# A shifted-window transformer block: attention output as one group per band in shared banks, both copies behind the second group, and a new order on all engines

## What is computed

```python
h = _ln(x, g1, b1)                                   # over the 128 channels
h = jnp.roll(h, (-3, -3), axis=(1, 2))
xw = _win_part(h)                                    # windows of 49 tokens
q, k, v = split(xw @ w_qkv + b_qkv)                  # 4 heads of 32
attn = einsum('whnd,whmd->whnm', q * 32 ** (-0.5), k)
attn = softmax(attn + bias[None] + MASK, axis=-1)    # relative bias, mask of the shift
out = einsum('whnm,whmd->whnd', attn, v) @ w_proj + b_proj
x = x + roll(_win_rev(out), (3, 3))
h2 = _ln(x, g2, b2)
h2 = gelu(h2 @ w_fc1 + b_fc1) @ w_fc2 + b_fc2        # 128 -> 512 -> 128
return x + h2
```

## Time and profile before

| | us |
|---|---|
| median of three runs | 3138.68 (3138.0 to 3142.47) |
| the profiled execution's own time | 3140.98 |
| its span, first to last instruction | 3139.2 |
| PE busy | 2989.0 (95%) |
| DVE busy | 2907.3 (93%) |
| ACT busy | 2255.3 (72%) |
| POOL busy | 1385.2 (44%) |

### The profile page before, as it was taken

How to read it: one execution, slowest core, us unless ns; L and a number is a source line. 1 busy time by engine, 2 the same in 40 slices (tenths; PEclk the granted TensorE clock), 3 DMA queues, 4 the chain that set the end, 5 groups by cost and what they waited for, 6 DMA issues and landing times.

```text
span 3139.2 us, 119115 instructions
## 1 busy us (share of the span) xinstructions
PE 2989.0 (95%) x51984; PEld 2732.5 (87%) x51984; DVE 2907.3 (93%) x7463; ACT 2255.3 (72%) x4480; POOL 1385.2 (44%) x775
## 2 busy tenths in 40 slices
PE   5999999999999999999999999999999999999998
PEld 3888888988888888889888888988888898888887
DVE  7999999999999999999999999999999999999995
ACT  3777777777777777777777777777777777777775
POOL 2444444444444444444444444444444444444442
PEclk9999999999999999999999999999999999999999
DMA  1111111111111111111111111111111111111110
GB/s 54 33 33 33 33 43 33 33 40 37 33 35 42 33 33 33 44 33 33 40 37 33 33 43 34 33 33 44 33 33 42 35 33 33 40 36 34 33 28 22
DMA packets 217571, 111.78 MB, mean 36 GB/s; under 512 B 15095, under 2 KB 216791, under 8 KB 217047
## 3 DMA queue, kind: packets, MB, share of 16 engines
q1 hardware_dynamic: 216899, 104.14, 13.0%
q10 hardware_dynamic: 147, 0.02, 0.0%
HBM read 52.73 MB, written 51.38 MB: 33 GB/s over the span
## 4 chain that ended last, share of the span: by engine, by line
PE 59%; DVE 29%; ACT 9%; issue 3%; SPq 0%; DMA 0%; POOL 0%; POOLq 0%; DVEq 0%; ACTq 0%
PE psum L767 13%; PE psum L725 7%; DVE xn L556 7%; PE psum L692 6%; PE psum L727 5%; PE psum L726 5%; DVE scores L576 5%; PE psum L699 4%; PE psum L746 4%; PE psum L753 4%; PE psum L707 3%; PE psum L720 3%; PE psum L732 3%; ACT probs L356 3%; DVE stream L590 3%
## 5 line engine op out<-in xcount | busy, mean ns | idle before, releaser
L318 POOL TENSOR_TENSOR rstd<-ve,minus_half 112x7 f32<-112x7 f32 x256 | 380.3, 1486 | 1251.7 <-DVE ve L551 1251.7
L767 PE MATMUL psum<-wfc,hT 128*112 128x128 f32 x7168 | 803.5, 273 | 1.5 <-ACT hT L410 1.5
L767 PEld LDWEIGHTS psum<-wfc,hT 128*112 128x112 f32 x7168 | 791.2, 177 | 2.1 <-issue 2.1
L410 ACT ACTIVATE hT<-psum,bias_h 128x392 f32<-128x392 f32 x1024 | 573.7, 599 | 233.0 <-PE psum L727 232.9
L314 POOL TENSOR_TENSOR probs<-probs,row_inv 128x784 f32<-128x784 f32 x256 | 383.7, 1521 | 470.7 <-DVE row_inv L585 470.7
L576 DVE TENSOR_TENSOR scores<-scores,row_max 128x784 f32<-128x784 f32 x256 | 447.5, 1748 | 8.8
L725 PE MATMUL psum<-x2T_hi,wfc_hi 128*128 128x392 f32 x1024 | 405.6, 396 | 28.0 <-DVE stream L590 25.8
L590 DVE TENSOR_TENSOR stream<-psum,stream 112x384 f32<-112x384 f32 (+1 forms) x512 | 303.9, 602 | 97.2 <-PE psum L753 83.3
L556 DVE TENSOR_SCALAR xn<-stream,mean,rstd 112x128 f32<-112x128 f32 x896 | 375.4, 476 | 1.6 <-POOL rstd L318 1.6
L321 POOL TENSOR_TENSOR stream<-stream,brow_fc 112x896 f32<-112x896 f32 x128 | 360.3, 2815 | 5.6 <-DVE xn L556 5.6
L402 ACT ACTIVATE kT<-psum,bias_k 128x392 f32<-128x392 f32 x256 | 150.8, 589 | 289.0 <-PE psum L732 285.6
(11 more groups left out here) (77 smaller groups left out, 5785.4 us busy)
## 6 DMA issues: line engine op xcount, KB each, us to landing
x_in<-in_x SPq DMA_DIRECT2D x224, 168.0 KB
out<-stream SPq DMA_DIRECT2D x224, 168.0 KB
x_in<-in_x SPq DMA_DIRECT2D x224, 17.5 KB
out<-stream SPq DMA_DIRECT2D x224, 17.5 KB
x_in<-in_x SPq DMA_DIRECT2D x224, 10.5 KB
out<-stream SPq DMA_DIRECT2D x224, 10.5 KB
x_in<-in_x SPq DMA_DIRECT2D x32, 96.0 KB
out<-stream SPq DMA_DIRECT2D x32, 96.0 KB
```

Source lines behind the costliest of these rows:

```text
L410: act.activation(hT[:, chunk, band * BAND:(band + 1) * BAND], tok_psum(c)[:, 0:BAND], ACT.Gelu, bias=bias_h[:, chunk:chunk + 1]).then_inc( ...
L767: last = pe.matmul(tok_psum(h)[0:TOK, (t - t0) * C:(t - t0 + 1) * C], hT[:, chunk, t * TOK:(t + 1) * TOK], wfc2[:, chunk, :], start=chunk ...
```

## The change

The work is the same, instruction for instruction, and so are the sizes. Four things move.

1. `attend` becomes `attend(band)`, with a semaphore for each band and a band's O in its own columns of the same two banks. ACT's `copy_o(band)` is called for both bands behind the wait for the second group.
2. The banks of q, k and v are dealt out anew, and PE, DVE and ACT are written in a new order. LEAD becomes 2.
3. DVE normalises all 7 tiles of `xn2` in one piece, straight behind both `inverse_sums`, and all 7 tiles of `xn1` in one piece. `stats1` moves to the start of the step, and the small `mean_var` for `xn1` to just ahead of `stats2`.
4. On POOL, `power` for `xn1` comes first in the step and `add_row` of the output bias second; `add_row` with the projection's bias now belongs to the step itself and stands right behind the two `normalise_probs`. DVE waits for it (`x_biased`) ahead of the residual add.

```diff
-LEAD, LAG = 3, 2
+LEAD, LAG = 2, 2
...
-        V_BANK, Q_BANK, K_BANK = (1, 1), (0, 0), (0, 0)
+        V_BANK, Q_BANK, K_BANK = (0, 1), (0, 1), (1, 0)
...
-        def o_psum(parity):
-            return psum[:, QKVO_BANK + parity, 0:BANDS * PAIRS * N]
+        def o_psum(band, parity):
+            return psum[:, QKVO_BANK + parity, band * PAIRS * N:(band + 1) * PAIRS * N]
...
             def step(n):
+                if has(n + 2):
+                    wait(pool, var1_ready, upto(n + 2))
+                    power(rstd1, ve1, rstd1_ready)
                 if has(n - 2):
...
                     add_row(n - 2, stream, brow_fc2, x1_biased)
...
                     normalise_probs(1)
-                if has(n + 3):
-                    wait(pool, var1_ready, upto(n + 3))
-                    power(rstd1, ve1, rstd1_ready)
-                if has(n + 2):
-                    wait(pool, x_loaded[(n + 2) % STEPS], dma_count((n + 2) % STEPS, (n + 2) // STEPS))
...
-                    add_row(n + 2, x_in, brow_proj, x_biased)
+                    wait(pool, x_loaded[n % STEPS], dma_count(n % STEPS, n // STEPS))
...
+                    add_row(n, x_in, brow_proj, x_biased)
...
+                    wait(act, o_made[1], upto(n))
+                    copy_o(0)
+                    copy_o(1)
...
+                if has(n + 2):
+                    wait(dve, raw1_done, upto(n + 2))
+                    mean_var(raw1, part1, mean1, ve1, raw1_done, parts1_done, stats1_done, var1_ready, upto(n + 2))
...
+                if has(n - 1):
+                    wait(dve, rstd2_ready, upto(n - 1))
+                    normalise(xn2, stream[:, (n - 1) % STEPS, :, :], mean2, rstd2, xn2_ready, 1)
+                    normalise(xn2, stream[:, (n - 1) % STEPS, :, :], mean2, rstd2, xn2_ready, 0)
...
+                    attend(0)
+                    wait(pe, probsT_copied[1], 2 * upto(n))
+                    attend(1)
...
+                    wait(pe, o_copied[1], upto(n))
...
+                if has(n):
+                    wait(pe, out_added[0], upto(n - 1))
...
                     transpose_tiles(xn2, 0, x2T_made)
```

More of the change, by code:

```diff
@@ L366, in copy_probsT, with copy_o @@
                                    ACT.Copy).then_inc(probsT_copied[band], 1)
-            def copy_o():
+            def copy_o(band):
+                image = oT[:, :, band, :].rearrange("c i (a w j) -> c w a i j", w=2, j=WIN)
                 for parity in range(2):
[L370 to L375, removed]
+                    last = act.activation(image[:, parity, :, :, :],
+                                          o_psum(band, parity).rearrange("c (a i j) -> c a i j", i=WIN, j=WIN), ACT.Copy)
+                last.then_inc(o_copied[band], 1)
             def copy_x(k, h):
@@ L462, in step @@
                     exp(1)
[L463 to L466, removed]
                 if has(n + 2):
+                    wait(act, q_made[0], upto(n + 2))
+                    copy_q(0)
                     wait(act, k_made[0], upto(n + 2))
                     copy_k(0)
+                if has(n + 1):
+                    copy_probsT(n + 1, 0)
                 if has(n):
@@ L710, in transpose_probs, with attend @@
                     last.then_inc(probsT_made[band], 1)
[L712 to L716, removed]
-                            keys = slice(HALF * parity, HALF * parity + N)
-                            for h in range(HEADS):
-                                rows = slice(HD * h, HD * (h + 1))
-                                last = pe.matmul(o_psum(parity)[rows, cols], vs[keys, band, pair, rows],
-                                                 probsT[keys, band, h // 2, pair, h % 2, 0:N], start=True, stop=True)
-                last.then_inc(o_made, 1)
+            def attend(band):
+                for pair in range(PAIRS):
+                    cols = slice(pair * N, (pair + 1) * N)
+                    for parity in range(2):
+                        keys = slice(HALF * parity, HALF * parity + N)
+                        for h in range(HEADS):
+                            rows = slice(HD * h, HD * (h + 1))
+                            last = pe.matmul(o_psum(band, parity)[rows, cols], vs[keys, band, pair, rows],
+                                             probsT[keys, band, h // 2, pair, h % 2, 0:N], start=True, stop=True)
+                last.then_inc(o_made[band], 1)
             def product(made, w_hi, w_lo, x_hi, x_lo):
@@ L809, in step @@
+                if has(n + 2):
+                    wait(pe, v_copied[0], upto(n + 1))
+                    if n < -1:
+                        wait(pe, xT_copied[0], upto(n + 2))
+                    make_q(n + 2, 0)
+                    make_k(n + 2, 0)
+                if has(n - 1):
+                    wait(pe, gelu_done[4], upto(n - 1))
                     make_out(0)
-                    wait(pe, xT_copied[1], upto(n + 2))
                     make_out(1)
```

232 lines of the change are left out of this document (104 added, 128 removed).

## The result

The changed kernel takes 3634.51 us (median of four runs, 3634.24 to 3635.29) against 3139.05 us: a ratio of 1.158, with a 95% interval of 1.156 to 1.160. The prediction was 3405 us, with a range up to 3450. The direction was right, the size was about half.

What follows compares the result with a forecast made beforehand. PE and DVE both had almost no room; the new chain, with DVE held up by POOL, summed to 26.05 us plus 0.1 for breaks, 26.15 a step against 24.01 over 124 periods: 3405 us, range 3350 to 3450.

Steps and rivals of the forecast that it cites:

- (e): DVE, row sum to output add: seven xn2 tiles wait on three POOL instructions, 7.43 us, 3.1 of it collision.
- (c): DVE's mean_var and stream statistics: 2.99 us, plus 1.8 us for a small operation held up by POOL's add.
- The first rival: DVE's small mean_var operations are not held up by POOL, so (c) costs 0: 3268 us, chance 0.24.
- The sign that was given: In DVE's mean_var for xn1, the second operation would take some 2 us.
- (f): PE's breaks in attention, laid to late instruction blocks: 0.1 us a step left of 0.45, bounds 0 and 0.45.
- (b): PE from xn2's transposes through scores, attention and projection: 9.65 us; DVE waits, both residual adds done at 10.4.
- the attention part: Attention grouped by band on PE: worth nothing by itself, bounds 0 to 0.4 us a step later.
- The rival on the other side: DVE's xn2 tiles run through once one has passed, so (e) loses 3 us: about 3050 us, chance 0.18.

Runs made afterwards that it cites:

- the move of the add: Changed kernel with POOL's add of the output bias put ahead of the power for xn1 and released by the last xn1 tile: 3379.59 us.
- the fillers: Changed kernel with four unused matmuls of 392 columns ahead of PE's wait for the first output add: 3448.63 us.
- both moves: Changed kernel with POOL's projection-bias add held until DVE has copied v, and its output-bias add released by the last xn1 tile: 3043.28 us.

## Why the prediction was wrong

The lay-out of a step held in all its parts but one.

- **(e), 7.43 us from the row sum to the output add.** Measured 1553.99 - 1546.60 = 7.39. One tile for each POOL instruction holds for three in a row.
- **(c), mean_var held up by 1.8 us.** Measured 2.11 for 0.17, and the move of the add took it away. The first rival is out. The sign that was given, the second operation, was right in about a third of the steps (40 of 124); in 83 it was the third.
- **(f), breaks down to 0.1 us a step.** In the changed kernel no idle time of the matmul in attention is left that is worth a row. With the fillers, at a full clock, it is 11.3 us or 0.09 a step; with both moves it is 4.1 us in all:

```profile
PE psum L713 <- issue: 11.3, 32, 0.8
```

- **(b), the attention part.** "Worth nothing by itself" was nearly so: in the kernel with both moves the grouping gains 0.18 us a step. The bounds, 0 to 0.4 us later, were for ACT's copies of O; PE waits for these once in the whole changed kernel, 1.1 us, so they were at their lower end.
- **(b), PE's way to the projection: the step that failed.** Transposes, scores, products, attention and projection were put at 9.65 us from rows in which PE had been working all along. With fillers, the projection ends at 9.70 us behind the end of the wait (1504.14 to 1512.15 + 1.69), so the sum was right for a fast clock. In the changed kernel it is 1536.42 + 1.69 - 1527.11 = 11.0 us, 1.3 more in this step, and the run's mean of 1.47 a step has steps in it in which the low clock lasted longer. The prediction itself had PE idle for nearly 3 us just ahead of this stretch, and put the lower clock behind that idle time at nothing, without a reason. In the undisturbed step PE had paused for no more than 0.46 us. But the breaks of up to 1.8 us pointed there, and the trace of the kernel before could have answered: it has the clock at 0.50 behind a break of 1.25 us, as shown above.
- **The range.** Its upper end, 3450, had only the bounds of (b) and (f), and did not even add these up: 0.4 and 0.35 us a step more would be 3498. The cost of the clock, 1.47 us a step or 182 us, was outside every bound. The remaining 0.35 us a step (26.50 against 26.15) is 0.1 in (c), as 2.11 - 0.17 is 1.94, some 0.1 in DVE's handling of the projection, and the rest breaks, which the fillers brought back in part, and steps longer than the one laid out, which I have not parted further.
- **The rival on the other side** (3050 us, "decides as soon as the collisions sum to less than 2.5 us") was wrong for the changed kernel. With both moves the collisions sum to some 1.5 us, and 3043 us came out.

The Trainium skill (TensorE: Matmul & The Clock Gate, Part 1) says that activity is what holds the clock up and that idling brings it down. The windows above agree, with 0.53 behind an idle time of 3.2 us; and so does the run with the fillers, whose mean is 0.997.

## What to carry to other kernels

When an engine is off the bound, ask where its instructions now fall: here two adds on an engine that is busy 36% of the time decide between 3043 and 3634 us. When a forecast makes TensorE wait, price the wait and then the work behind it at the lower clock; unused matmuls in the gap are a quick test, and removing the wait is the cure. Where two engines take turns by whole instructions, a queue of short operations ends little before or after the queue of long ones beside it: to take three of seven tiles away gained 26 us, to take one of the three long ones away 424 us.

## What the runs showed of the hardware that I had not expected

- The clock falls behind pauses shorter than I would have feared: behind 3.2 us in 124 steps of 125 (to 0.53 and 0.51 in the windows shown), and behind 1.90 us in 80 of 124 and in 74 of 125, in two different kernels (mean 0.959 in both). The length of the pause does not decide alone. Behind pauses of 1.46 us in each step the mean stayed at 0.998, while in the kernel before the clock fell to 0.50 behind a break of 1.25 us in the middle of attention's small matmuls. What else decides, no run shows.
- An operation of 7 columns and two SBUF inputs is held up like one of 784: 2.11 us against 0.17 alone, where the subtraction took 2.55 against 0.97. In the changed kernel it is the third operation of the row in 83 steps and the second in 40, so some hundredths of a microsecond decide which one is caught.
- 4 tiles in 4.41 us and 7 in 5.19 us beside the same three POOL instructions.
